# Decay attention and a mixture of experts in one kernel: DMA transposes in place of TensorE transposes

## The reference

```
x = x + attn(layernorm(x)):
  q, k, v = split(x @ w_qkv);  q = elu(q)+1;  k = elu(k)+1
  running_kv, running_ksum = decay scans over time of k*v and k
  out = (q*running_kv / max(sum(q*running_ksum), 1e-6)) @ w_out
x = x + moe(layernorm(x)):
  scores = softmax(x @ gate_w);  top_k(scores, 2)
  g = silu(x @ w_gate[e]) * (x @ w_up[e])
  routed = sum over the two experts of weight * (g @ w_down[e])
  shared = silu(x @ sw_gate) * (x @ sw_up) @ sw_down
  out = routed + shared
```

## Time and profile before

| | |
|---|---|
| median of 3 runs | 745.48 us (744.18 to 746.0) |
| the profiled execution, its own time | 746.98 us |
| its span | 745.2 us |
| PE busy | 695.5 us, 93% |
| DVE busy | 477.7 us, 64% |
| ACT busy | 267.0 us, 36% |
| POOL busy | 232.1 us, 31% |
| mean granted TensorE clock | 0.983 of full speed |
| DMA | 72.48 MB, 97 GB/s over the span |

### The profile page before, as it was taken

How to read it: one execution, slowest core, us unless ns; L and a number is a source line. 1 busy time by engine, 2 the same in 40 slices (tenths; PEclk the granted TensorE clock), 3 DMA queues, 4 the chain that set the end, 5 groups by cost and what they waited for, 6 DMA issues and landing times.

```text
span 745.2 us, 12605 instructions
## 1 busy us (share of the span) xinstructions
PE 695.5 (93%) x4024; PEld 475.0 (64%) x4025; DVE 477.7 (64%) x855; ACT 267.0 (36%) x408; POOL 232.1 (31%) x308
## 2 busy tenths in 40 slices
PE   3979789999999899999999999999999999999992
PEld 2757477777777686666565665666666666666661
DVE  6879878987996753878788777643444444444341
ACT  4343321342342223565665665422222222222220
POOL 6100110102102014344352432234444444444431
PEclk9999999999999799999999999999999999999997
DMA  6830013202203248745465131234444444444443
GB/s 212 296 116 6 14 27 131 70 15 71 99 30 88 83 142 277 230 126 167 120 180 145 29 57 29 46 70 83 84 84 84 84 81 80 86 83 82 81 59 40
DMA packets 39413, 72.48 MB, mean 97 GB/s; under 512 B 4560, under 2 KB 12752, under 8 KB 39376
## 3 DMA queue, kind: packets, MB, share of 16 engines
q0 software_dynamic: 11680, 25.18, 19.8%
q1 hardware_dynamic: 25392, 42.62, 17.3%
q10 hardware_dynamic: 2304, 4.20, 1.7%
HBM read 48.65 MB, written 23.33 MB: 97 GB/s over the span
## 4 chain that ended last, share of the span: by engine, by line
PE 75%; DVE 13%; issue 4%; DMA 2%; ACT 2%; SPq 1%; POOL 1%; POOLq 0%; DVEq 0%; ACTq 0%
PE ps_y L470 17%; PE ps_g L470 16%; PE ps_u L470 16%; PE ring L353 15%; PE turn_x L457 3%; PE turn_h L490 3%; PE ps_gate L353 2%; DMA shared<-in_L_attn_w_out_dram 2%; DVE run_kv L1189 1%; DVE at_l L1231 1%; SPq L748 1%; DVE stats L1141 1%; PE turn L437 1%; DVE xn L1151 1%; DVE wq_l L1163 1%
## 5 line engine op out<-in xcount | busy, mean ns | idle before, releaser
L1268 DVE TENSOR_TENSOR hidT<-turn_h,hidT 128x384 f16<-128x384 f32 x71 | 39.5, 556 | 107.2 <-ACT hidT L1009 106.7
L353 PE MATMUL ring<-xnT_h,wq_h 128*128 128x512 f32 x192 | 79.7, 415 | 4.5 <-DVE xnT_l L1158 2.5
L806 POOL TENSOR_SCALAR var_eps<-mean_var 128x1 f32<-128x1 f32 x32 | 12.0, 376 | 230.0 <-DVE mean_var L1248 129.3
L470 PE MATMUL ps_y<-routed,hidT 128*128 x351 | 82.1, 379 | 1.3 <-DVE hidT L1268 1.3
L353 PE MATMUL ring<-xnT_l,wq_h 128*128 128x512 f32 x192 | 76.9, 400 | 0.0
L353 PE MATMUL ring<-xnT_h,wq_l 128*128 128x512 f32 x192 | 76.6, 399 | 0.0
L470 PE MATMUL ps_g<-routed,xT 128*128 x468 | 76.2, 313 | 0.0
L470 PE MATMUL ps_u<-routed,xT 128*128 x468 | 76.2, 313 | 0.0
L885 POOL DMA_INDIRECT out_dram<-y_job,idx_out x39 | 62.6, 1605 | 43.4 <-DVE y_job L1594 36.2
L892 POOL TENSOR_TENSOR squares<-squares 128x704 bf16<-128x704 bf16 (+1 forms) x24 | 45.4, 1892 | 98.4 <-ACT squares L971 98.4
L470 PE MATMUL ps_y<-shared,hidT 128*128 128x512 f16 x288 | 67.5, 379 | 5.9 <-DVE hidT L1268 5.5
(11 more groups left out here) (205 smaller groups left out, 1324.6 us busy)
## 6 DMA issues: line engine op xcount, KB each, us to landing
routed<-in_L_ffn_w_gate_dram SPq DMA_DIRECT2D x8, 704.0 KB, 4.5
routed<-in_L_ffn_w_up_dram SPq DMA_DIRECT2D x8, 704.0 KB, 8.1
x_res<-in_L_attn_x_dram SPq DMA_DIRECT2D x18, 256.0 KB, 3.0
out_dram<-x SPq DMA_DIRECT2D x16, 256.0 KB, 3.2
xn_scratch<-xn SPq DMA_DIRECT2D x16, 256.0 KB, 2.0
x_in<-xn_scratch ACTq DMA_DIRECT2D x16, 256.0 KB, 3.5
routed<-in_L_ffn_w_down_dram SPq DMA_DIRECT2D x8, 512.0 KB, 8.7
out_dram<-y_job POOLq DMA_DIRECT2D x16, 256.0 KB, 4.1
```

Source lines behind the costliest of these rows:

```text
L353: ins = pe.matmul(ps, a, b, start=(i == 0), stop=(i == len(steps) - 1))
L470: ins = pe.matmul(ps, a[i][:, k, :], w(j, k), start=(start and q == 0), stop=(stop and q == len(steps) - 1))
L1268: dve.tensor_tensor(hidT[:, 1], turn_h[:, 0:FC, :], hidT[:, 0], ALU.subtract).then_inc(s["hidT_s"], 1)
```

## The change

Three transposes on TensorE are replaced by transposing DMAs of 2-byte elements, all issued by SP.

**Hidden.** silu writes into hid itself, `hidden` multiplies in place, ScalarE casts the upper half and VectorE the rest into `hid_hl` (fp16, 2 x 384 columns, padded with zeros once), and `turn_hidden` on SP turns it into `hidT[b]`, of which there are two. The upper half of a unit waits until the transposition of the unit before has landed.

**Rows of x.** `norm_2` scales rows by 2048, ScalarE (`hi_2`) and VectorE (`lo_2`) make fp16 halves `xn2_hl` (128 x 1024), which go as such to the scratch tensor. `turn_tile` turns a tile of it straight into xT; for jobs the indirect DMA gathers rows into `x_job`, and `turn_gathered` turns those.

**Gate.** `turn_rows` turns `xn2_hl` into xg_even or xg_odd. gate_w gets a power-of-two scale of its own (`gate_norms`, `gate_scale`) and fp16 halves side by side; a tile is 4 matmuls of 16 columns and 4 of 8. `logit_un` undoes the scale.

**Moved with it.** The last block's expand and output use other PSUM banks, so that gate and up products of unit 1 can come before them; gates of tiles 13 to 15 come in units 1 and 2. Expert 0 is loaded from POOL's queue, experts 1 to 7 from ScalarE's within the units, since SP now waits for hid. NORM_UNIT goes from 2 to 3, SPLIT_UNIT from 7 to 8, the routing starts one unit later. In attention phi of q is made in place, so ScalarE's next exp of q waits for num_s instead of phiq_s.

Core of the diff:

```diff
-            def turn_hidden(u, first=False):
-                pe.wait_ge(s["hid_s"], u + 1)
-                if not first:
-                    pe.wait_ge(s["hidT_s"], u)
-                for c, col in enumerate(FCOL):
-                    ins = pe.transpose(turn_h[:, c, :], hid[:, col:col + P], ident[:, :])
-                ins.then_inc(s["turned_h"], 1)
-
-            def down_product(u, t, w, start, stop, first=False):
-                pe.wait_ge(s["hidT_s"], u + 1)
+            def down_product(u, b, t, w, start, stop, first=False):
+                pe.wait_ge(s[f"hT{b}"], 8 * (u - b) + 16)
...
             def gate(t):
...
-                ins = split_product(ps_gate[:, t * E:(t + 1) * E],
-                                    [((xn2T_h[:, k, :], xn2T_l[:, k, :]), (gw_h[:, k, :], gw_l[:, k, :]))
-                                     for k in chunks])
+                for k in chunks:
+                    pe.matmul(ps_gate[:, at:at + 2 * E], xg[:, k, :], gw_hl[:, k, :], start=(k == 0), stop=False)
+                for k in chunks:
+                    ins = pe.matmul(ps_gate[:, at:at + E], xg[:, KC + k, :], gw_hl[:, k, 0:E], start=False,
+                                    stop=(k == KC - 1))
...
+            def turn_rows(t):
                 sp.wait_ge(s["xn2_s"], t + 1)
...
+                if t >= 2:
+                    sp.wait_ge(s["gate_mm"], t - 1)
+                sp.dma_start_transpose((xg_even if t % 2 == 0 else xg_odd)[:, :, :], xn2_hl[:, t % 2, :])\
+                    .then_inc(s[f"xg{t % 2}"], 16)
...
+            def turn_tile(t):
+                sp.wait_ge(*tile_sem("xn2_out", t))
...
+                sp.dma_start_transpose(xT[:, t % 2], xn2_d[t * P:(t + 1) * P, :]).then_inc(s[f"xin{t % 2}"], 16)
+
+            def turn_hidden(u, b=None):
...
+                    sp.wait_ge(s["tables_s"], 1)
+                    sp.wait_ge(s["d_mm"], free)
+                    sp.wait_ge(s["hidl_s"], ready)
+                sp.dma_start_transpose(hidT[:, b], hid_hl[:, :, :].rearrange("p h c -> p (h c)")).then_inc(s[f"hT{b}"], 16)
+
+            def turn_gathered(r, b):
+                here, free = sp.to_reg(8 * (r - b) + 16), sp.to_reg(HALVES * NT + r - 1)
...
+                sp.wait_ge(s[f"gin{b}"], here)
+                sp.wait_ge(s["u_mm"], free)
+                sp.dma_start_transpose(xT[:, b], x_job[:, b, :]).then_inc(s[f"xin{b}"], 16)
...
+            with sp.Fori(0, (JOBS - 3) // 2) as i:
+                turn_hidden(UNITS + 2 * i, 0)
+                turn_gathered(2 * i + 2, 0)
+                turn_hidden(UNITS + 2 * i + 1, 1)
+                turn_gathered(2 * i + 3, 1)
...
+            def upper_hid(u, b, first=False):
+                act.wait_ge(s["hid_s"], u + 1)
...
+                    act.wait_ge(s[f"hT{1 - b}"], 8 * (u + b))
+                act.copy(hid_hl[:, 0, 0:F], hid[:, :]).then_inc(s["hidh_s"], 1)
...
+                for e in range(1, E):
+                    if u == max(3 * (e - 1), 4):
+                        act.wait_ge(s["over_0"], 2)
+                        load_expert(act, e)
...
+            def rest_hid(u):
+                dve.wait_ge(s["hidh_s"], u + 1)
+                dve.tensor_tensor(hid_hl[:, 1, 0:F], hid[:, :], hid_hl[:, 0, 0:F], ALU.subtract).then_inc(s["hidl_s"], 1)
```

More of the change, by code:

```diff
@@ L41, in preln_decay_attention_moe @@
     FC = (F + P - 1) // P
-    FCOL = [P * c for c in range(FC - 1)] + [F - P]
-    OVER = P * FC - F
+    LAST = F - P * (FC - 1)
+    OVER = P - LAST
     TOPK = 2
@@ L180, in preln_decay_attention_moe @@
         tab_a = esb("tab_a", [P, NT, E])
+        tri = esb("tri", [P, P])
+        ones = esb("ones", [P, P])
         score = esb("score", [P, NT, E])
@@ L655, in _ @@
                 gate_product(u + 1, t_next, t_next % 2, gate_w)
-                turn_hidden(u, u == 0)
                 up_product(u + 1, t_next % 2, up_w)
-                if half == 0 and t < NT - 1:
-                    turn_tile(t + 1, (t + 1) % 2)
-                elif half == 0:
-                    turn_gathered(0, 0)
-                elif t == NT - 1:
-                    turn_gathered(1, 1)
+                if u == 1:
+                    gate(last + 1)
+                if u == 2:
+                    gate(last + 2)
+                    gate(last + 3)
                 if norm_unit(u - 1) is not None:
                     column_norms(norm_unit(u - 1))
-                if u == 4:
+                if u == RANK_UNIT:
                     rank_tokens()
@@ L910, in _ @@
                 gather(r, r % 2, first=r < 2)
+                if r == 0:
+                    for u in range(2 * (NT - AHEAD + 1), HALVES * NT):
+                        if norm_unit(u) is not None:
+                            fold(norm_unit(u))
                 if r < AHEAD - 1:
@@ L939, in phi_parts @@
                 if i:
-                    act.wait_ge(s["phik_s" if which == 0 else "phiq_s"], i)
+                    act.wait_ge(s["phik_s" if which == 0 else "num_s"], i)
                 z = ring[item(n, c) % RING]
@@ L1003, in gate_silu @@
                 if not first:
-                    act.wait_ge(s["hid_s"], u)
-                act.activation(silu[:, :], ps_g[:, 0:F], ACT.Silu, scale=by).then_inc(s["silu_s"], 1)
-            def upper_hidT(u, first=False):
-                act.wait_ge(s["turned_h"], u + 1)
-                act.copy(hidT[:, 0], turn_h[:, 0:FC, :]).then_inc(s["hidTh_s"], 1)
+                    act.wait_ge(s["hidl_s"], u)
+                act.activation(hid[:, :], ps_g[:, 0:F], ACT.Silu, scale=by).then_inc(s["silu_s"], 1)
+            def upper_hid(u, b, first=False):
+                act.wait_ge(s["hid_s"], u + 1)
+                if first:
+                    act.wait_ge(s["pads"], 1)
+                else:
+                    act.wait_ge(s[f"hT{1 - b}"], 8 * (u + b))
+                act.copy(hid_hl[:, 0, 0:F], hid[:, :]).then_inc(s["hidh_s"], 1)
             def move_y(t, b, first=False):
-                act.wait_ge(s["y_mm"], t + 1)
+                act.wait_ge(s["d_mm"], HALVES * (t + 1))
                 if not first:
@@ L1070, in _ @@
             shared_by = silu_scale[:, E:E + 1]
-            first = (NB - 2) * TPB
-            upper_xT(0, 0)
-            move_xn2T(first)
+            before_last = (NB - 2) * TPB
+            last = (NB - 1) * TPB
+            hi_2(before_last + 1)
             gate_silu(0, shared_by, True)
-            move_xn2T(first + 1)
+            upper_hid(0, 0, True)
+            hi_2(before_last + 2)
             for c in chunks:
                 hi_a(NB - 1, c)
-            for t in range(first + 2, NT - 1):
-                move_xn2T(t)
             gate_silu(1, shared_by)
-            upper_hidT(0)
-            move_xn2T(NT - 1)
-            upper_xT(1, 1)
-            load_job_x(2, 0)
-            load_job_x(3, 1)
-            for u in range(1, HALVES * NT):
+            hi_2(before_last + 3)
+            upper_hid(1, 1)
+            hi_2(last)
+            hi_2(last + 1)
+            gate_silu(2, shared_by)
+            hi_2(last + 2)
+            upper_hid(2, 0)
+            hi_2(last + 3)
+            move_y(0, 0, first=True)
+            for u in range(2, HALVES * NT):
                 t, half = u // 2, u % 2
@@ L1395, in _ @@
                 query(n, 0)
+                tile_before(lo_2, 2, 2)
                 max_step(n * KC)
@@ L1603, in _ @@
                        HALVES * NT - 2: job_weights}
-            for u in range(1, HALVES * NT):
-                t, half = u // 2, u % 2
-                rest_hidT(u)
+            for u in range(2, HALVES * NT):
                 if u + 1 < HALVES * NT:
```

510 lines of the change are left out of this document (270 added, 240 removed).

## The result

Median 779.1 us (776.1 to 785.2, 4 runs) against 745.7 us in the same session; ratio 1.045, 95% interval 1.042 to 1.048. I had forecast 710.

A forecast was written before the change was run, and what follows sets the result against it. TensorE, busy 93% of the span, was taken as the bound. Blocks 2 and 3 -7, last block's end -9, shared expert -14, jobs -7, end +1 sum to -36 us: 710 predicted, range 698 to 722.

The forecast's parts named there:

- T = 4.0: Time in us of a transposing DMA from issue to landing, set from plain loads with a median of 3.3.
- R = 1.9 + T: Path in us from the end of an up product to its down product: 1.9 before the DMA's issue, then its landing.
- The scatters' floor: In the jobs, each scatter waits for the one before: 5.90 us a job at least, with landing of 4.5 to 5.0.
- The shared expert, -14: 31 units of the shared expert: 17.6 us less from transposes, 1.8 back for gates and 1.8 for loads; bounds -20 and +271.
- rival of the late transposition: Turned hid is late for every down product, T above 5.6; 854 us at T = 7.1; chance 18%.
- it catches up; together 1.8 us: Shared expert: ScalarE, busy 116 of 204 us, absorbs the expert loads' issues at 0.33 us each; cost 1.8 us.
- The jobs, -7: The 39 jobs go from 6.29 to 6.1 us each, 7 us less; bounds 15 less to 24 more.
- rival of the scatters: Scatter landings in the jobs grow by 0.8 to 1.0 us, period 6.7 to 6.9; 732 to 739 us; chance 15%.
- The last block's end, -9: Last attention block's end: cheaper gate tiles save 10.4 us, expand starts about 4 us later; bounds -14 and 0.
- Blocks 2 and 3, -7: Attention blocks 2 and 3: eight cheaper gate tiles take 8.6 us off TensorE, 7 counted; bounds -9 and 0.
- As fast as a plain one: The skill's statement on transposing DMAs; by it T would be 3.3 us and hid wholly hidden.
- block by block: Rival: DMA turns 128x128 blocks one after another at 0.84 us each, 11.8 us a job; about 1000 us; chance 7%.

The follow-up runs named there:

- e4: Changed kernel with the transposing DMAs of hid and x made plain DMAs of the same bytes (values not the reference's): 738.6 us, 0.990 of before.
- e2: Changed kernel with all eight expert loads issued from SP's queue again: 755.2 us, 1.012 of before.
- e7: e4 and e2 together: plain DMAs for hid and x, all expert loads on SP: 732.8 us, 0.981 of before.
- e12: e10 with the expert loads as in the changed kernel, expert 0 by GpSimd, the others by ScalarE: 749.8 us, 1.005 of before.
- e6: e5 with all expert loads issued by SP, as in e2: 755.9 us, 1.013 of before.
- e5: Changed kernel with hid transposed by TensorE again; x and gate keep transposing DMAs, loads keep their queues: 750.0 us, 1.006 of before.
- e9: Changed kernel with a plain DMA of the same bytes for hid only, x still transposed by DMA: 749.5 us, 1.003 of before.
- e8: e6 with plain DMAs of the same bytes for the rows of x (values not the reference's): 732.9 us, 0.983 of before.
- e10: Changed kernel with TensorE turning every hid, and x from tile 3 on, all expert loads on SP: 746.4 us, 1.000 of before.
- e13: Changed kernel with hid and the jobs' x turned by TensorE, x of shared tiles still by DMA: 737.5 us, 0.989 of before.
- e1: Changed kernel with ScalarE loading expert 2 at unit 6 and expert 3 at unit 7, instead of 4 and 6: 779.9 us, 1.045 of before.

## Why the prediction was wrong

The steps, as the prediction put them:

**T = 4.0.** Right as a median: 4.1. **R = 1.9 + T.** Right: 1.96 us before the issue. **The scatters' floor.** Right: landing 4.7/5.0/5.3 us, and 5.91 a job in e4.

**The shared expert, -14: failed, +44.6.** This is the step that decided the result. Two sentences failed. One was "I go by the median, since that load had five others around it": the transpositions of the first units had the expert loads around them just so, and landed after up to 12.7 us. My rival of the late transposition (18%) had this mechanism, but for every unit; it held for some, where the loads ran. The other was "it catches up; together 1.8 us". I priced a load's issue at 0.33 us from the row of the x loads; behind other large loads one pair took 2.38 and the next 4.36. The expert loads' own issues were in the trace of the kernel before, and one took 4.2 us (on SP, where nothing that TensorE waited for in the units stood behind it):

```profile
L777 SPq DMA_DIRECT2D routed<-in_L_ffn_w_down_dram x16: 480/738/4202, 282.7 to 393.5; - x16
```

And I priced what is queued on ScalarE at nothing: the squares for the column norms stand there behind the loads, behind the landing of expert 0, and behind the cast of the next unit's hid, and TensorE waited 28.9 us for them. The price of the loads' queues was 24 us beside turned hid (e2), 6 beside plain bytes (e7), 3 with all turned by TensorE from tile 3 on (e12), and -6 with hid by TensorE and x by the DMA (e6 against e5). The price of hid's new way without turning is left in e4 and e9: 25 us of waits for the squares. A common root is that I never counted the DMA engines' time. The share of the earlier trace rows was 0.47 on average, with the loads bunched in parts of it; 17 MB of loads were to share the engines with one and a half turning DMAs a unit, each at about twice the plain price. The windows after have 0.91 and 0.99 there. The other is that I counted the way of hid only as TensorE's wait, and not as ScalarE's.

**The jobs, -7: failed, +6.7.** The formula took one T for all. T lay between 2.7 and 5.9 us; a late one costs its excess and an early one returns nothing, since the scatters' chain or TensorE is then the bound. TensorE waited 19.2 us for it, 25.4 us idle in all, and ran 223.5 us where 39 x 5.52 is 215. Of these 8 us some 3 are half clock, which it had twice for 3.4 us, after waits of 2.0 and 2.1 us; the rest I did not trace. The rival of the scatters had "landing grows" and got the sign of the stretch, but its landing grew by 0.2 us in the kernel after, not by 0.8 to 1.0. It did in e5 and nearly in e6. Why e5's scatters land at 5.6 us with the engines at 0.67, and the kernel after's at 5.0 with 0.89, is open; that the transpositions of x cause the late landing in e6 is shown by e8.

**The last block's end, -9: right in kind, -11.6.** A gate tile took less than the 0.6 us I gave it (timeline, after):

```profile
248.33 0.28 PE L494 MATMUL ps_gate<-gw_hl,xg_odd 128*128 128x16 f16 x4 [5.36 <-DMA xg_odd<-xn_hl]
248.46 0.25 PE L496 MATMUL ps_gate<-gw_hl,xg_odd 128*128 128x8 f16 x4
248.64 1.22 PE L469 MATMUL turn<-den,of_head 32*128 32x512 f32 x1
```

8 matmuls in 0.31 us. The wait ahead of expand was 5.36 us, and expand began at 248.6, where I had 250.7. But e10 shows that this win moved work: it is given back in the next units. In e13, where x comes by DMA there, nearly nothing is (205.7 against 203.7).

**Blocks 2 and 3, -7: failed, -0.9.** "VectorE has 14.6 us of room there" is an average over the stretch. Its busy time went from 96.1 to 98.0 us, TensorE's from 108.4 to 100.0, and the stretch hardly changed. The experiments edit nothing ahead of this point, and in their profiles it is reached at 234.9 to 238.1 us against 238.9 before: a gain of 1 to 4 us, not 7. That VectorE, 89% busy, takes the rest is my reading; no run isolates it.

**As fast as a plain one, and block by block.** In jobs, the transposing DMA of x took 1.55 us of the 16 engines against 0.71 for the same bytes (e6, e8), and that of hid landed after 4.1 us against 3.3 (medians of the kernel after and of e4). The Trainium skill, in "Advanced Engine Details and Errata", section "X-Bar Transpose (TRN2)", says that transposing DMAs are as fast as regular ones; here they are not, and the measurement decides. The rival of blocks one after another did not come true either: the six blocks of hid landed in 2.7 us at best. By the 1309 ns that the Trainium skill, "VectorE: DVE Perf Modes", section "The three transpose paths", gives for one block, six in a row would be 7.9 us, an estimate from that page's figure.

**A row that I set badly.** In the earlier trace rows the landing of 13.2/13.7/14.2 us is not that of the fills printed above it, which landed after 3.2/4.1/7.3 us. It is that of the last two loads of the shared expert's down weights at 26 us, the load that the prediction means by 14.2.

## What to carry to other kernels

Before moving work onto DMAs, sum the DMA engines' time stretch by stretch, with small packets at their own price, and look at the fullest stretch, not at the mean. Take a landing time from the stretch in which the DMA will run, with its spread, and ask what is queued behind each new issue, and behind each new wait, on its engine. And when a change has parts, price each in each stretch: here the transposition of x paid in the shared stretch and cost in the jobs, that of silu x up cost in the shared stretch and paid nowhere clearly, and the best kernel took each part only where it pays.

## What was not expected of the hardware

- A transposing DMA moves its bytes in packets under 512 B: 39,072 for 9.70 MB, against 5,328 for the plain ones of e8, at 2.2 times the engines' time. SP spent 1.21 to 1.26 us on its issue, against 0.46 for the same 192 KB plain (e4) and 0.33 for a plain one on ScalarE.
- An issue can be held: 4.36 us for two on ScalarE in the kernel after, 4.07 and 7.02 for one each on SP in e6, 4.20 for one on SP in the kernel before, all behind expert loads.
- Expert 0's loads from GpSimd landed after 7.8, 13.6, 14.9 and 15.0 us in the profile of the kernel after, but after 6.4, 8.3, 9.0 and 8.9 us in e1, which is the same program up to there. In e13, where hid was not turned by DMA beside them, they took 5.8, 7.0, 7.0 and 7.9. No other profile has it above 8.9, with hid turned by DMA or not; so the 15.0 is of this one run, and what causes it is open.
